# A decoder layer on one core: head outputs and the output weights of the first attention as fp16 high and low parts

## The chip, the cores and the metric

One core of one Trainium2 chip runs the whole layer. The time is device microseconds from launch to end; the median of three runs is compared. The engines are named as in the profile: PE (TensorE, its matmuls), PEld (its weight loads), DVE (VectorE), ACT (ScalarE), POOL (GpSimd) and SP (SyncE, which issues all DMAs of this kernel). PSUM is the matmuls' output memory, SBUF the memory of tiles.

## The reference, cut to what matters

The layer is: latent self-attention with 128 heads of 4 content and 64 rope dimensions, cross-attention with 32 heads, a feed-forward layer with LoRA experts, each behind a layer norm and with a residual sum. x is 8 x 128 x 512, fp32. What is changed is the last line of the first attention:

```python
    scores = (einsum('bqhd,bkhd->bhqk', q_c, k_c) + einsum('bqhd,bkd->bhqk', q_r, k_r)) / scale
    attn = jax.nn.softmax(scores, axis=-1)
    out = jnp.einsum('bhqk,bkhd->bqhd', attn, v_c)
    out = out.reshape(b, s, N_HEADS * HEAD_DIM)      # 512 columns
    return out @ Wo                                  # 512 x 512, then x = x + this
```

## The kernel before

**The loop over half steps.** The 128 heads go in 32 groups of 4 (`g`), each in two half steps (`t` = 0, 1) of four batches, so there are 64 half steps `h = 2g + t`. In half step h, PE projects the rope queries of job h (24 matmuls in 8 pieces, `project`), computes rough scores of job h-1 in four pieces (`rough_scores`, L1547) and full scores of job h-2 (L1580, L1581), turns the row maxima of job h-1 (`max_turn`, L1557) and weighs the values of job h-3 (L1595). All engines run the same half steps, each in its own written order, tied by semaphores. A job's scores need its row maxima back as a row of the query tile QC: DVE takes the maxima (`row_max`, L1095), PE turns them, DVE writes them to mT (`max_out`, L1164), and SP copies mT into QC.

**DVE in a half step** (`half`): `q_low` of job h-1, chunk 1 (two L1083), `o_out` (L1170), four `row_max` (L1095), `q_low` of job h, chunk 0 (two L1083), and last `max_out` of job h-1. PE's third rough piece of a half step waits for the first `row_max` of the same half step, since they share two PSUM banks. **ACT in a half step**: `q_high` of job h-1, chunk 1, four casts to Ph (L935), four exponentials (L928), with `q_high` of job h, chunk 0 among them. **POOL** forms Pl, the low part of the probabilities (L653, four in each half step), and in each even half step splits the next group's weights: `high` (L628), after the Pl of one job `rest` (L632, L634), then a copy of values (L639).

**The normalisation of head outputs.** Jobs store unnormalised outputs and softmax sums to HBM; SP gathers them per quarter T of the heads (32 heads, 128 rows) into U (outputs, turned, fp32) and SU (sums). DVE takes the reciprocal of SU and multiplies, 128x128 for each of eight batches b. The table `shares(h)` places these: `inverse_sums` (L1202) among the row maxima, `apply_sums` (L1207) behind the second `q_low`, ahead of `max_out`. Quarter 0 falls on half steps 26 to 33, quarter 1 on 42 to 49, quarter 2 on 58 to 63 and just behind. Quarter 3 is done by `normalise` (L1213, L1214) after the last half step and, for batches 4 to 7, within the cross-attention.

**The product with Wo.** `output_part(v, T)` (L1620) and `output(v, T)` (L1629) multiply U by the fp32 weights wo_sb: 32 products of 128x128 by 128x512. The first twelve stand between the rough and full scores of the last jobs; then come eight for batches 0 and 1, eight for 2 and 3, and four single ones in the cross-attention. `x1_part` and `x1` add them to the residual xs; norm statistics and `norm_rows` (tile pn) of the next layer norm follow on DVE.

**The code of each engine** is either written out (`spelled`) or a hardware loop of two groups per pass (`looped`). DVE and ACT have groups 1 and 2 written out and loop from 3.

## Time and profile before

| what | value |
|---|---|
| median of 3 runs | 836.3 us (836.21 to 837.79) |
| the profiled execution | 836.2 us, its span 834.5 us |
| PE busy | 795.2 us, 95% |
| DVE busy | 627.3 us, 75% |
| POOL busy | 590.8 us, 71% |
| ACT busy | 582.8 us, 70% |
| mean granted TensorE clock | 0.997 |

The span is the time between the first and the last instruction, and 1.7 us lie around it. Busy time is summed over the span. Rows of the timeline give the start, the length, the engine, the line and the operation; the bracket behind is idle time of the engine ahead of the row, and what ended it. An instruction that has been issued and waits inside the engine for a port has a longer row and no bracket.

### The profile page before, as it was taken

What the parts mean: (1) busy time and instruction counts of PE and PEld (TensorE: products, weight loads), DVE (VectorE), ACT (ScalarE), POOL (GpSimd) and SP (SyncE); (2) the same over time, 40 slices, a digit from 0 to 9 for tenths busy, and PEclk for the clock granted to TensorE, in tenths of its full rate; (3) what the DMA queues carried; (4) which work ended last, traced back from release to release, by engine and by line L of the source; (5) the groups of instructions that cost most, each with busy time, mean ns of one, the idle gap of its engine ahead of it and who ended that gap; (6) DMA issues with size and microseconds to landing.
All of it is one profiled execution on the core that took longest, in us unless ns stands there. A gap on an engine that the chain in (4) does not pass through costs nothing.

```text
span 834.5 us, 17885 instructions
## 1 busy us (share of the span) xinstructions
PE 795.2 (95%) x5641; PEld 391.1 (47%) x5641; DVE 627.3 (75%) x1189; ACT 582.8 (70%) x1072; POOL 590.8 (71%) x535
## 2 busy tenths in 40 slices
PE   5999999999999999999999999999999888999986
PEld 3464444444444444444444444444434434545443
DVE  6767676676766888767788877688868868888755
ACT  8757777777777778777777777768765556556641
POOL 6967999999987888878888788868657334222110
PEclk9999999999999999999999999999999999999999
DMA  9345355534343333433334434452322000000001
GB/s 339 124 170 146 88 160 145 171 82 97 101 123 103 79 95 84 117 106 91 102 88 93 106 91 105 100 153 56 81 57 65 2 2 2 14 14 15 15 14 38
DMA packets 52177, 75.80 MB, mean 91 GB/s; under 512 B 10257, under 2 KB 34097, under 8 KB 51617
## 3 DMA queue, kind: packets, MB, share of 16 engines
q1 hardware_dynamic: 52128, 75.23, 32.8%
q8 instruction: 22, 0.36, 0.2%
q14 instruction: 27, 0.21, 0.1%
HBM read 38.69 MB, written 19.40 MB: 70 GB/s over the span
## 4 chain that ended last, share of the span: by engine, by line
PE 82%; DVE 7%; ACT 4%; issue 3%; SPq 2%; DMA 1%; POOL 0%; DVEq 0%; ACTq 0%
PE PS L1508 38%; PE PS L1442 7%; PE PS L1547 7%; PE PS L1580 7%; PE PS L1581 6%; PE PS L1595 5%; DVE xm L1281 1%; PE PS L1620 1%; PE PS L1741 1%; PE PS L1557 1%; PE PS L1707 1%; PE PS L1815 1%; PE PS L1629 1%; SPq L464 1%; PE PS L1748 1%
## 5 line engine op out<-in xcount | busy, mean ns | idle before, releaser
L1508 PE MATMUL PS<-XTh,W 128*128 128x512 f16 x1024 | 346.2, 379 | 0.0
L653 POOL TENSOR_TENSOR Pl<-PR,Ph 128x512 f16<-128x512 f32 x254 | 286.3, 1159 | 29.8 <-ACT Ph L935 29.8
L928 ACT ACTIVATE PR<-PS 128x512 f32<-128x512 f32 x256 | 152.8, 597 | 129.5 <-PE PS L1581 122.6
L1095 DVE TENSOR_REDUCE mneg<-PS 128x4 f16<-128x512 f32 x256 | 171.6, 685 | 34.7 <-PE PS L1547 33.0
L1508 PE MATMUL PS<-XTl,W 128*128 128x512 f16 x512 | 193.8, 379 | 0.0
L1083 DVE SCALAR_TENSOR_TENSOR QS<-PS,QC 64x512 f16<-64x512 f32 x256 | 175.4, 685 | 20.9 <-ACT QC L845 16.8
L845 ACT ACTIVATE QC<-PS 64x512 f16<-64x512 f32 x256 | 150.7, 589 | 9.2 <-PE PS L1508 4.3
L1508 PEld LDWEIGHTS PS<-XTh,W 128*128 128x128 f16 x1024 | 96.5, 97 | 118.8 <-issue 25.9
L935 ACT ACTIVATE Ph<-PR 128x512 f16<-128x512 f32 x256 | 139.2, 617 | 0.0
L1547 PEld LDWEIGHTS PS<-KC,QC 112*128 112x128 f16 x1024 | 78.4, 97 | 63.5 <-DVE mneg L1095 2.8
L1547 PE MATMUL PS<-KC,QC 112*128 112x128 f16 x1024 | 99.5, 219 | 0.8 <-ACT QC L845 0.7
L1580 PE MATMUL PS<-QC,KC 113*128 113x512 f16 x256 | 97.8, 382 | 2.1 <-DMA QC<-mT 1.6
L1581 PE MATMUL PS<-QS,KS 128*128 128x512 f16 x256 | 97.3, 380 | 0.0
L628 POOL TENSOR_TENSOR W<-Wraw,wscale 128x1024 f16<-128x1024 f32 x30 | 56.8, 1893 | 46.2 <-PE PS L1508 40.6
L1508 PEld LDWEIGHTS PS<-XTl,W 128*128 128x128 f16 x512 | 49.8, 97 | 46.3
L1164 DVE TENSOR_SCALAR mT<-PS 16x128 f16<-16x128 f16 x64 | 13.6, 212 | 76.7 <-PE PS L1557 76.7
L784 POOL TENSOR_TENSOR rstd<-rstd,power 128x1 f32<-128x1 f32 x16 | 8.8, 553 | 82.4 <-DVE rstd L1260 82.4
L634 POOL TENSOR_TENSOR W<-Wraw,W 128x1024 f16<-128x1024 f32 x30 | 64.0, 2133 | 2.4
L632 POOL TENSOR_TENSOR Wraw<-Wraw,wscale 128x1024 f32<-128x1024 f32 x30 | 56.8, 1892 | 0.2
L1170 DVE COPY OS<-PS 128x512 f32<-128x512 f32 x64 | 44.2, 691 | 4.1 <-PE PS L1595 2.2
L1281 DVE TENSOR_REDUCE xm<-PS 128x4 f16<-128x512 f32 x64 | 41.0, 682 | 2.0 <-PE PS L1707 2.0
L1595 PE MATMUL PS<-Ph,Vg 128*32 128x512 f16 x512 | 41.4, 383 | 0.0
(229 smaller groups left out, 1032.4 us busy)
## 6 DMA issues: line engine op xcount, KB each, us to landing
Wraw<-in_wqr SPq DMA_DIRECT2D x32, 512.0 KB, 4.8
QS<-QC SPq DMA_DIRECT2D x64, 256.0 KB, 3.1
head_outputs<-OS SPq DMA_DIRECT2D x256, 40.0 KB
q_content_parts<-stg SPq DMA_DIRECT2D x12, 256.0 KB, 2.9
k_content_parts<-stg SPq DMA_DIRECT2D x12, 256.0 KB, 3.1
QC<-q_content_parts SPq DMA_DIRECT2D x116, 24.0 KB
KC<-k_content_parts SPq DMA_DIRECT2D x29, 96.0 KB
xs<-in_x SPq DMA_DIRECT2D x8, 256.0 KB, 5.2
```

What stands on the lines that cost most here:

```text
L634: nc.gpsimd.tensor_tensor(Wl[:, par], Wraw[:, par], Wh[:, par], ALU.subtract).then_inc(s_ws, 1)
L653: nc.gpsimd.tensor_tensor(Pl[:, 4 * j.s + b], PR[:, b], Ph[:, 4 * j.s + b], ALU.subtract).then_inc(s_pl, 1)
L845: nc.scalar.activation(QC[0:RD, j.p, j.s, 2 * c + h, :], PS[RD * h:RD * (h + 1), bQ[c], :], ACT.Copy, scale=1 / WS).then_inc(s_qh, 1)
L928: nc.scalar.activation(PR[:, b, :], PS[:, bB[b % 2], :], ACT.Exp, scale=ATT_SCALE).then_inc(s_e, 1)
L935: nc.scalar.activation(Ph[:, 4 * j.s + b, :], PR[:, b, :], ACT.Copy).then_inc(s_ph, 1)
L1083: nc.vector.scalar_tensor_tensor(QS[0:RD, j.p, j.s, i, :], PS[RD * h:RD * (h + 1), bQ[c], :], 1 / WS, QC[0:RD, j.p, j.s, i, :], ALU.mult, ...
L1095: nc.vector.tensor_reduce(mneg[:, j.p, j.s, :, b], PS[:, bA[b % 2], :].rearrange("p (j k) -> p j k", j=GH), AX.X, ALU.max, negate=True).th ...
L1508: last = mm(PS[:, bQ[c], :], wt[:, j.w, k, c * P:(c + 1) * P], xt[:, k, sl], start=(i == 0), stop=(i == 3 * KT - 1))
L1547: last = mm(PS[:, bA[i % 2], h * S:(h + 1) * S], QC[0:MROW, j.p, j.s, h, i * S:(i + 1) * S], kc(j.k)[0:MROW, b * S:(b + 1) * S], start=Tru ...
L1580: mm(to, kc(j.k)[0:MROW + 1, b * S:(b + 1) * S], QC[0:MROW + 1, j.p, j.s, :, i * S:(i + 1) * S], start=True, stop=False)
L1581: mm(to, KS[:, b * S:(b + 1) * S], QS[:, j.p, j.s, :, i * S:(i + 1) * S], start=False, stop=True).then_inc(s_b, 1)
L1595: last = mm(PS[32 * b:32 * (b + 1), bO, :], Vg[:, j.p, part, 4 * j.s + b, :], probs[:, 4 * j.s + b, :], start=(n == 0), stop=(n == 2))
```

## The change

wo_sb goes; in its place stand wo_h and wo_l, fp16, of together the same size. The weights land in bw_raw; at the end of half steps 9 and 10 ACT writes half of wo_h (128x1024) and DVE then writes half of wo_l, ahead of its `max_out`. The feed-forward weights, which used bw_raw too, are loaded as before but wait for wo_l. U is read as fp16 pairs in place (Uparts): DVE multiplies into SU, casts to the high part and subtracts for the low part. In the last quarter ACT casts (`u_high`) and DVE subtracts (`u_low`). Each fp32 product becomes three fp16 ones: high by wo_h, high by wo_l, low by wo_h, and the residual sum multiplies by 1/WS. ACT and DVE have groups 1 to 6 written out and loop from 7.

```diff
         scratch = top[0]
-        wo_sb = sb("wo_sb", [P, KT, DM])
+        wo_h = sb("wo_h", [P, KT, DM], F16)
+        wo_l = sb("wo_l", [P, KT, DM], F16)
         wx_raw = sb("wx_raw", [P, KT, DM])
...
         SU = sb("SU", [P, TOK])
+        Uparts = U[:].rearrange("p k t -> p (k t)").bitcast(F16).rearrange("p (k b n s) -> p k b n s", k=KT, n=2, s=S)
         KC2 = sb("KC2", [P, 2, TOK], F16)
...
         s_wdh, s_wds = sem("wd_high"), sem("wd_split")
-        s_c, s_ce, s_cl, s_kc = sem("c_ready"), sem("c_high"), sem("c_low"), sem("k_copied")
+        s_c, s_kc = sem("c_ready"), sem("k_copied")
+        s_ce, s_cl = sem("high_of_c_wo_and_last_u"), sem("low_of_c_wo_and_last_u")
         s_u, s_uh, s_ul, s_uv = sem("up_ready"), sem("up_high"), sem("up_low"), sem("v_high")
...
             sp.wait_ge(s_vl, B)
-            for g, (t, d, done) in enumerate(((wo_sb, wo, s_wo), (wx_raw, xwq, s_wx), (xwo_sb, xwo, s_ffn), (bw_raw, bw, s_ffn))):
+            for g, (t, d, done) in enumerate(((bw_raw, wo, s_wo), (wx_raw, xwq, s_wx), (xwo_sb, xwo, s_ffn), (bw_raw, bw, s_ffn))):
                 spelled(half, 3 + g, 3 + g)
+                if g == 3:
+                    sp.wait_ge(s_cl, 6 + 2)
                 sp.dma_start(t[:], d).then_inc(done, 16)
...
                         q_high(J(0), 0)
-            spelled(half, 1, 2)
-            looped(act, half, 3, G0 - 1)
+                if isinstance(g, int) and 2 * g + t in (9, 10):
+                    k = 2 * (2 * g + t - 9)
+                    act.wait_ge(s_wo, 16)
+                    nc.scalar.activation(wo_h[:, k:k + 2], bw_raw[:, k:k + 2], ACT.Copy, scale=WS).then_inc(s_ce, 1)
+            def u_high(b):
+                act.wait_ge(s_un, B * (KT - 1) + b + 1)
+                nc.scalar.activation(Uparts[:, KT - 1, b, 0], SU[:, b * S:(b + 1) * S], ACT.Copy).then_inc(s_ce, 1)
+            spelled(half, 1, 6)
+            looped(act, half, 7, G0 - 1)
             spelled(half, G0, NG - 1)
...
                 p_high(job(n))
+            u_high(0)
+            u_high(1)
             act.wait_ge(s_red, 2)
...
                 turned_out(u)
+                if u - 1 in SUMS_AT:
+                    u_high(SUMS_AT[u - 1])
                 if r == 2 and 0 <= b + 1 < B:
...
                         split_high(n)
+                    u_high(2)
+                    u_high(3)
                     nc.scalar.activation(ex[:, 0:1], power[:], ACT.Exp)
...
                         apply_sums(*piece)
+                if h in (9, 10):
+                    k = 2 * (h - 9)
+                    dve.wait_ge(s_ce, 6 + h - 8)
+                    nc.vector.scalar_tensor_tensor(wo_l[:, k:k + 2], bw_raw[:, k:k + 2], WS, wo_h[:, k:k + 2],
+                                                   ALU.mult, ALU.subtract).then_inc(s_cl, 1)
                 max_out(J(1))
...
                 dve.wait_ge(s_dch, chain[0])
-                nc.vector.tensor_tensor(U[:, T, sl], U[:, T, sl], SU[:, sl], ALU.mult).then_inc(s_un, 1)
+                link(nc.vector.tensor_tensor(SU[:, sl], U[:, T, sl], SU[:, sl], ALU.mult))
+                link(nc.vector.tensor_copy(Uparts[:, T, b, 0], SU[:, sl]))
+                nc.vector.tensor_tensor(Uparts[:, T, b, 1], SU[:, sl], Uparts[:, T, b, 0], ALU.subtract).then_inc(s_un, 1)
+            def u_low(b):
+                dve.wait_ge(s_ce, 8 + b + 1)
+                nc.vector.tensor_tensor(Uparts[:, KT - 1, b, 1], SU[:, b * S:(b + 1) * S], Uparts[:, KT - 1, b, 0],
+                                        ALU.subtract).then_inc(s_cl, 1)
             def normalise(T, b):
...
                 link(nc.vector.reciprocal(SU[:, sl], SU[:, sl]))
-                nc.vector.tensor_tensor(U[:, T, sl], U[:, T, sl], SU[:, sl], ALU.mult).then_inc(s_un, 1)
-            spelled(half, 1, 2)
-            looped(dve, half, 3, 12)
+                if T < KT - 1:
+                    link(nc.vector.tensor_tensor(SU[:, sl], U[:, T, sl], SU[:, sl], ALU.mult))
+                    link(nc.vector.tensor_copy(Uparts[:, T, b, 0], SU[:, sl]))
+                    nc.vector.tensor_tensor(Uparts[:, T, b, 1], SU[:, sl], Uparts[:, T, b, 0], ALU.subtract).then_inc(s_un, 1)
+                else:
+                    nc.vector.tensor_tensor(SU[:, sl], U[:, T, sl], SU[:, sl], ALU.mult).then_inc(s_un, 1)
+            spelled(half, 1, 6)
+            looped(dve, half, 7, 12)
             spelled(half, 13, 16)
...
                 dve.wait_ge(s_o0, v - B // 2 + 1)
-                nc.vector.tensor_tensor(xs[:, v, :], xs[:, v, :], PS[:, v - B // 2, :], ALU.add).then_inc(s_x0, 1)
+                nc.vector.scalar_tensor_tensor(xs[:, v, :], PS[:, v - B // 2, :], 1 / WS, xs[:, v, :], ALU.mult, ALU.add).then_inc(s_x0, 1)
...
                     dve.wait_ge(s_x0, v - B // 2 + 1)
-                nc.vector.tensor_tensor(xs[:, v, :], xs[:, v, :], PS[:, o1_bank(v), :], ALU.add).then_inc(s_x1, 1)
+                nc.vector.scalar_tensor_tensor(xs[:, v, :], PS[:, o1_bank(v), :], 1 / WS, xs[:, v, :], ALU.mult, ALU.add).then_inc(s_x1, 1)
...
             normalise(KT - 1, 1)
+            u_low(0)
+            u_low(1)
             x1(0)
...
                     normalise(KT - 1, 3)
+                    u_low(2)
+                    u_low(3)
                 if u == FIRST + 3:
...
                     normalise(KT - 1, SUMS_AT[u])
+                if u - 1 in SUMS_AT:
+                    u_low(SUMS_AT[u - 1])
...
+            def residual(bank, v, T, start, stop):
...
+                for n, (part, wt) in enumerate(((0, wo_h), (0, wo_l), (1, wo_h))):
+                    if n == 2 and T == KT - 1:
+                        pe.wait_ge(s_cl, 8 + v + 1)
+                    last = mm(PS[:, bank, :], Uparts[:, T, v, part], wt[:, T, :], start=(start and n == 0), stop=(stop and n == 2))
+                return last
             def output_part(v, T):
...
                 pe.wait_ge(s_un, B * T + v + 1)
-                last = mm(PS[:, v - B // 2, :], U[:, T, v * S:(v + 1) * S], wo_sb[:, T, :], start=(T == 0), stop=(T == KT - 2))
+                last = residual(v - B // 2, v, T, T == 0, T == KT - 2)
                 if T == KT - 2:
...
-                pe.wait_ge(s_un, B * T + v + 1)
+                if T < KT - 1:
+                    pe.wait_ge(s_un, B * T + v + 1)
+                else:
+                    pe.wait_ge(s_ce, 8 + v + 1)
                 if T == 0:
                     pe.wait_ge(s_x0, v + 1)
-                last = mm(PS[:, o1_bank(v), :], U[:, T, v * S:(v + 1) * S], wo_sb[:, T, :], start=(T == 0 or v >= B // 2),
-                          stop=(T == KT - 1))
+                last = residual(o1_bank(v), v, T, T == 0 or v >= B // 2, T == KT - 1)
                 if T == KT - 1:
...
-            pe.wait_ge(s_wo, 16)
+            pe.wait_ge(s_cl, 6 + 2)
             for i in range(4):
...
```

The order of instructions on DVE at the end of half step 26 and the start of 27, the first with a piece of quarter 0 (U the outputs, SU the sums, mneg the row maxima, QS and QC query tiles, OS a job's outputs). Before:

```order
L1095 TENSOR_REDUCE mneg<-PS 128x4 x2
L1083 SCALAR_TENSOR_TENSOR QS<-PS,QC 64x512 x2
L1207 TENSOR_TENSOR U<-U,SU 128x128
L1164 TENSOR_SCALAR mT<-PS 16x128
L1083 SCALAR_TENSOR_TENSOR QS<-PS,QC 64x512 x2
L1170 COPY OS<-PS 128x512
```

and now:

```order
L1114 TENSOR_REDUCE mneg<-PS 128x4 x2
L1102 SCALAR_TENSOR_TENSOR QS<-PS,QC 64x512 x2
L1231 TENSOR_TENSOR SU<-U,SU 128x128
L1232 CAST U<-SU 128x128
L1233 TENSOR_TENSOR U<-SU,U 128x128
L1183 TENSOR_SCALAR mT<-PS 16x128
```

Two instructions more stand between the second `q_low` and `max_out`. The same place in half step 9, now written out:

```order
L1114 TENSOR_REDUCE mneg<-PS 128x4 x4
L1102 SCALAR_TENSOR_TENSOR QS<-PS,QC 64x512 x2
L1218 SCALAR_TENSOR_TENSOR wo_l<-bw_raw,wo_h 128x1024
L1183 TENSOR_SCALAR mT<-PS 16x128
L1102 SCALAR_TENSOR_TENSOR QS<-PS,QC 64x512 x2
```

Before, the loop had the same four without the row of wo_l. DVE behind the last scores, with `normalise` of batches 0 and 1 of quarter 3 and `x1(0)`. Before:

```order
L1170 COPY OS<-PS 128x512
L1213 RECIPROCAL SU<-SU 128x128
L1214 TENSOR_TENSOR U<-U,SU 128x128
L1213 RECIPROCAL SU<-SU 128x128
L1214 TENSOR_TENSOR U<-U,SU 128x128
L1332 TENSOR_TENSOR xs<-xs,PS 128x512
L1258 BN_STATS stats<-xs 128x6
```

and now:

```order
L1189 COPY OS<-PS 128x512
L1245 RECIPROCAL SU<-SU 128x128
L1251 TENSOR_TENSOR SU<-U,SU 128x128
L1245 RECIPROCAL SU<-SU 128x128
L1251 TENSOR_TENSOR SU<-U,SU 128x128
L1237 TENSOR_TENSOR U<-SU,U 128x128 x2
L1369 SCALAR_TENSOR_TENSOR xs<-PS,xs 128x512
```

The two subtractions of `u_low` stand ahead of the residual sum of batch 0.

## Rows read from the trace of the kernel before

**Rows 1.** The page: busy time, share of the span and instructions of each engine.

```profile
PE 795.2 (95%) x5641; PEld 391.1 (47%) x5641; DVE 627.3 (75%) x1189; ACT 582.8 (70%) x1072; POOL 590.8 (71%) x535
```

**Rows 2.** PE's timeline 155 to 174: turns of the row maxima (start, length).

```profile
155.43 0.22 PE L1557 MATMUL PS<-turns,mneg 128*16 128x128 f16 x1
...
164.17 0.22 PE L1557 MATMUL PS<-turns,mneg 128*16 128x128 f16 x1
...
173.13 0.22 PE L1557 MATMUL PS<-turns,mneg 128*16 128x128 f16 x1
```

**Rows 3.** DVE's timeline 155 to 167: the first `q_low` of two half steps.

```profile
156.16 1.41 DVE L1083 SCALAR_TENSOR_TENSOR QS<-PS,QC 64x512 f16<-64x512 f32 x2 [0.26 <-ACT QC L845]
...
165.28 1.41 DVE L1083 SCALAR_TENSOR_TENSOR QS<-PS,QC 64x512 f16<-64x512 f32 x2 [0.55 <-ACT QC L845]
```

**Rows 4.** The chain that ended last, 690 to 834.5: two stretches.

```profile
751.81 2.59 PE PS L1442 x12
754.40 0.86 PE PS L1815 x2
```

**Rows 5.** Groups by line and form: busy us, mean ns | idle before.

```profile
L1629 PE MATMUL PS<-wo_sb,U 128*128 128x512 f32 x40 | 18.8, 601 | 0.2 <-DVE U L1214 0.2
...
L1207 DVE TENSOR_TENSOR U<-U,SU 128x128 f32<-128x128 f32 x23 | 12.9, 564 | 0.0
...
L1620 PE MATMUL PS<-wo_sb,U 128*128 128x512 f32 x24 | 12.6, 605 | 0.0
...
L1244 DVE SCALAR_TENSOR_TENSOR Wxl<-wx_raw,Wxh 128x2048 f16<-128x2048 f32 x1 | 2.3, 2285 | 0.0
...
L945 ACT ACTIVATE W<-Wraw 128x1024 f16<-128x1024 f32 x2 | 2.1, 1050 | 3.1 <-DMA Wraw<-in_wqr 3.1
```

**Rows 6.** DVE's timeline 277 to 288: behind half steps 26 and 27.

```profile
277.17 1.09 DVE L1207 TENSOR_TENSOR U<-U,SU 128x128 f32<-128x128 f32 x1
278.65 0.21 DVE L1164 TENSOR_SCALAR mT<-PS 16x128 f16<-16x128 f16 x1 [0.39 <-PE PS L1557]
279.12 1.41 DVE L1083 SCALAR_TENSOR_TENSOR QS<-PS,QC 64x512 f16<-64x512 f32 x2 [0.26 <-ACT QC L845]
...
287.38 0.21 DVE L1164 TENSOR_SCALAR mT<-PS 16x128 f16<-16x128 f16 x1 [1.20 <-PE PS L1557]
```

**Rows 7.** POOL's timeline 276 to 281.

```profile
276.22 1.89 POOL L632 TENSOR_TENSOR Wraw<-Wraw,wscale 128x1024 f32<-128x1024 f32 x1
278.19 2.13 POOL L634 TENSOR_TENSOR W<-Wraw,W 128x1024 f16<-128x1024 f32 x1
280.26 0.45 POOL L639 COPY Vg<-V 128x320 f16 x1
```

**Rows 8.** DVE's timeline 568 to 571: end of half step 59.

```profile
569.11 0.32 DVE L1207 TENSOR_TENSOR U<-U,SU 128x128 f32<-128x128 f32 x1
569.76 0.21 DVE L1164 TENSOR_SCALAR mT<-PS 16x128 f16<-16x128 f16 x1 [0.33 <-PE PS L1557]
```

**Rows 9.** POOL's timeline 568 to 572.

```profile
569.36 1.16 POOL L664 TENSOR_TENSOR W<-Wraw,W 128x512 f16<-128x512 f32 x1
```

**Rows 10.** ACT's timeline 128 to 129: end of half step 9.

```profile
128.13 0.60 ACT L928 ACTIVATE PR<-PS 128x512 f32<-128x512 f32 x1 [0.49 <-PE PS L1581]
```

**Rows 11.** DVE's timeline 117 to 150: `max_out` of half steps 9 and 10.

```profile
129.03 0.21 DVE L1164 TENSOR_SCALAR mT<-PS 16x128 f16<-16x128 f16 x1 [1.49 <-PE PS L1557]
...
138.31 0.21 DVE L1164 TENSOR_SCALAR mT<-PS 16x128 f16<-16x128 f16 x1 [1.49 <-PE PS L1557]
```

**Rows 12.** POOL's timeline 128 to 131.

```profile
128.88 1.89 POOL L628 TENSOR_TENSOR W<-Wraw,wscale 128x1024 f16<-128x1024 f32 x1 [1.03 <-issue]
```

**Rows 13.** DVE's timeline 623 to 628.

```profile
624.70 1.25 DVE L1214 TENSOR_TENSOR U<-U,SU 128x128 f32<-128x128 f32 x1
...
627.16 0.69 DVE L1332 TENSOR_TENSOR xs<-xs,PS 128x512 f32<-128x512 f32 x1
```

**Rows 14.** POOL's timeline 585 to 668.

```profile
623.53 4.62 POOL L653 TENSOR_TENSOR Pl<-PR,Ph 128x512 f16<-128x512 f32 x4 [2.49 <-ACT Ph L935]
```

## The prediction

> **What bounds the kernel now.** I read the page first: PE is busy for 95% of the span, DVE for 75% [rows 1]. Then PE's timeline at the one instruction that comes once in a half step, the turn of the row maxima: two stand 8.74 us apart [rows 2], which most of the 64 half steps repeat, and PE has no gap in between. So the loop is PE's, and in a half step that lasts longer another engine ends a wait last. How little is spare shows the next turn, 8.96 us behind [rows 2]: in that half step DVE began its first `q_low` 1.11 us after the turn instead of 0.73 [rows 2, 3], at a place where its loop jumps back. DVE was 0.38 us late and PE lost 0.22. The order explains it: behind `q_low` come `o_out` and the first `row_max`, and PE's third rough piece waits for that one. So **what delays DVE's end of a half step by more than 0.16 us costs PE the rest.** The 0.4 to 1.5 us that DVE idles before `max_out` are the only cover.
>
> **What the products gain.** An fp32 product is two matmul rows that take 0.86 us together, 0.43 each; twelve fp16 ones of 512 columns take 2.59 us, 0.216 each [rows 4]. Three of those take 0.65, so each of the 32 products (64 rows of L1620 and L1629 [rows 5]) takes 0.21 less: 6.8 us of PE time at most. Twelve stand among the last scores, where PE is the bound: 12 x 0.21 = 2.5. I take 2.2, since the first three are followed by rough pieces that wait for row maxima. The other twenty stand where DVE is next (below).
>
> **What the normalisation costs in the loop.** DVE had one multiplication for each piece. It now has a chain of three: multiplication, cast, subtraction. The last is of the multiplication's kind and size, 0.3 us when alone. Of such a cast there is no row; it lies between nothing and that 0.3, and I take 0.2, since it reads one tile less. In an odd half step that is 0.5 more against 1.20 us of idle time before `max_out` [rows 6]: no cost. In an even one the multiplication lasts 1.09 us and only 0.39 stay idle [rows 6]. The cause is on POOL's timeline: L632 runs from 276.22 to 278.11 [rows 7], and the multiplication, issued at 277.17, ends at 278.26, 0.15 behind it. Over all 23 its mean is 0.564 [rows 5]: that is eight of 1.04 (the even half steps of quarters 0 and 1) and fifteen of 0.3. So a DVE instruction with both inputs in SBUF waits until the POOL instruction that runs is done.
>
> The Trainium skill (SBUF — State Buffer, "Who interferes with whom") says that the two engines share one pair of ports, held for a whole instruction, and that a DVE instruction with two SBUF inputs contends with POOL's reads. By the same section a cast in a two-port mode contends too. The first is what the row shows; for the second no row of before exists. By the rule the second end below holds, 2.2 us for each piece.
>
> At 278.19 POOL starts L634, 2.13 us, to 280.32, and at its end the copy L639, 0.45 us [rows 7]. The multiplication's row ends at 278.26, so nothing of the chain gets ahead of L634. The two ends of the cost:
> - Only the subtraction waits: it ends at 280.32 + 0.15 = 280.47 and `max_out` follows at once (before: 278.65). `q_low` starts 0.25 us after that, at 280.75 instead of 279.12 [rows 6]: 1.63 late, 1.5 for PE.
> - The cast, issued at 278.3, waits as the multiplication did: it ends at 280.45, L639 may get in between (to 280.9), the subtraction ends at 281.2, `q_low` starts at 281.45: 2.3 late, 2.2 for PE.
>
> I take **2.0 us in each of eight even half steps, 16 us**, range 12 to 17.5; it is nearer the second end, as the cast is issued under L634 just as the multiplication is under L632. It repeats, since POOL's part of an even half step begins when PE is done with a projection: a stall of PE moves both. The maxima's way into QC is late by the same amount and lies beside the same stall.
>
> Quarter 2 meets other work of POOL. In half step 59 the multiplication starts at 569.11, lasts 0.32, and `max_out` starts at 569.76; POOL has L664 from 569.36 to 570.52 [rows 8, 9] and the next of the pair of about the same length behind it. Cast behind the first, subtraction behind the second: done at 571.8, 2.0 after the old `max_out`, 1.9 for PE. Half step 58 is alike, but the one behind it waits for transfers already: 0.3. Half step 62 does two pieces, 1.0 more against 0.4 of idle time: 0.4. Half steps 60, 61 and 63 have cover. Together **2.6**, range 1 to 3.5.
>
> **What splitting the weights costs.** At the end of half step 9 ACT's last exponential ends at 128.73 [rows 10]. Behind it comes the cast of wo_h, 1.05 us by the row of its size [rows 5], to 129.8. DVE, which did `max_out` at 129.03 [rows 11], waits for it, and then for POOL's L628, 128.88 to 130.77 [rows 12], two SBUF inputs again. A subtraction of this form over 2048 columns took 2.29 us [rows 5], 1.2 for half of it. It ends at 131.95, `max_out` is 2.9 late. PE then loses 2.7 us, of which 0.55 were lost there before (9.28 between two `max_out`, the first jump back of DVE's loop [rows 11]): 2.1 net. At half step 10 POOL has got behind and holds nothing at that moment: ACT 1.1 and DVE 1.2 us behind the turn, 2.0 late, 1.9 for PE. Together **4.0**, range 2.5 to 4.7. That the loops start at group 7 takes away two jumps back (half steps 10 and 14) and makes that of half step 18 the first: nothing on balance. The later load of the feed-forward weights costs nothing: SP comes to it when DVE is past half step 10, and their first reader stands behind the loop.
>
> **The end of the first attention.** Behind the twelve products DVE is next. The multiplication of batch 0 lasts 1.25 us under POOL's four Pl, which go on from 623.53 to 628.15, and `x1(0)` starts at 627.16 [rows 13, 14]. Now two subtractions stand ahead of it, the first held by the fourth Pl: `x1(0)` at 628.75, **1.6** later, and the norm, the query projection and the cross-attention are behind it. For batches 2 and 3 the subtractions wait for ACT, which has three weight splits ahead of its casts, and for POOL: between 0.6 (their own length) and 2.2 (two of POOL's instructions of 1.1), I take **1.5**; PE's faster products there are hidden by DVE. Batches 4 to 7 give DVE 0.3 more and PE 0.21 less each: **0.3** in all. Less the 2.2 gained, this end costs 1.2, range -2 to 3.
>
> **Sum.** 16 + 2.6 + 4.0 + 1.2 = 23.8 us on the 836.2 of the profiled execution: 860. The median of the three runs is 0.1 higher, which changes nothing. With all ends of the terms: 850 to 865.
>
> **Rivals.**
> - *Only the subtraction is held* (the cast runs beside POOL). Eight times 1.5 instead of 2.0: 856. For it: the cast reads one tile. Chance 0.28, against 0.55 for the forecast as it stands.
> - *DVE's chain slips past POOL.* For it: the multiplication of batch 0 got in between two Pl instructions of POOL [rows 13, 14]. If cast and subtraction took the 0.08 us between L632 and L634 and held L634 off, an even half step would be late by 0.5 - 0.39, under 0.16: nothing. Against it: L634 begins before the multiplication's row ends. Left are 4.0 for the weights, 0.5 in quarter 2 and 1.2: 842. Chance 0.07.
> - *The saving on PE decides: faster.* One mechanism: DVE's additions stay hidden. It decides where DVE is less than 0.16 us late at half steps 9 and 10 and at the ten even pieces; then 6.8 are left, 829, or the 2.2 alone, 834. For it: 25% of DVE's span is idle. Against it: that idle time is 0.39 where it counts. Chance 0.06.
> - *A second stall behind the first*: late maxima also keep SP from its stores and content loads, and the next half step stalls as well. One more microsecond at ten places: 870. Against it: no row shows a half step in which SP's queue is the one waited for. Chance 0.04.
>
> **How the numbers follow.** The forecast is 860, its own range 853 to 866. For 8 in 10 the range takes in the case of the subtraction alone and part of the last: 848 to 868. A change under 0.2% (1.7 us) is about what a measurement of this kernel can't tell from none. Slower 0.9, the same 0.04 (cases that cancel), faster 0.06.
>
> **What would show it.** In the profile after, the turn of half step 27 comes 10.7 us behind that of 26 instead of 8.74, likewise behind each even half step of quarters 0 and 1, and 8.74 behind the odd ones. In the even ones the cast's row lasts about 2 us, to L634's end (or the subtraction's, in the second case). At half step 9 DVE's `wo_l` row lasts over 2 us. PE is idle ahead of L1547 for DVE's row maxima. The products of 0.65 us show as shorter stretches among the last scores. The forecast is wrong if DVE's chain in an even half step ends before L634 does, or if PE's third rough piece has more slack than the 0.16 us that I read from one late half step.

## The result, and the profile after

| | before | after |
|---|---|---|
| median of 4 runs each, side by side | 837.0 us (836.2 to 840.0) | 858.3 us (856.3 to 862.2) |
| ratio | | 1.026 (1.0236 to 1.0284) |
| profiled execution, its span | 836.2, 834.5 us | 856.3, 854.6 us |

The changed kernel is 2.6% slower. The page's busy times beside [rows 1]:

```profile
PE 790.5 (93%) x5673; PEld 387.2 (45%) x5673; DVE 664.1 (78%) x1247; ACT 585.8 (69%) x1082; POOL 591.2 (69%) x535
```

PE is busy for 4.7 us less and DVE for 36.8 us more (rows in which DVE waits for POOL count as busy), in a span that is 20.1 us longer. In PE's timeline the turns of the row maxima (now L1600) show where the time went. These are the turns and the waits of PE for row maxima in the changed kernel, 127 to 151 and 280 to 300 us:

```profile
128.49 0.22 PE L1600 MATMUL PS<-turns,mneg 128*16 128x128 f16 x1
134.62 0.40 PE L1590 MATMUL PS<-KC,QC 112*128 112x128 f16 x4 [1.99 <-DVE mneg L1114]
139.69 0.22 PE L1600 MATMUL PS<-turns,mneg 128*16 128x128 f16 x1
144.89 0.40 PE L1590 MATMUL PS<-KC,QC 112*128 112x128 f16 x4 [1.06 <-DVE mneg L1114]
149.78 0.22 PE L1600 MATMUL PS<-turns,mneg 128*16 128x128 f16 x1
...
280.83 0.22 PE L1600 MATMUL PS<-turns,mneg 128*16 128x128 f16 x1
286.25 0.40 PE L1590 MATMUL PS<-KC,QC 112*128 112x128 f16 x4 [1.39 <-DVE mneg L1114]
291.13 0.22 PE L1600 MATMUL PS<-turns,mneg 128*16 128x128 f16 x1
299.87 0.22 PE L1600 MATMUL PS<-turns,mneg 128*16 128x128 f16 x1
```

The intervals behind half steps 9 and 10 are 11.20 and 10.09 us, the one behind half step 26 is 10.30, the one behind 27 is 8.74 as before [rows 2]. Each of the long ones, and each one behind the other even half steps of quarters 0 and 1, has an idle stretch of PE (1.06 to 1.99 us) that a row maximum ended. Taken over all turns and the first events behind them, the 20.1 us are:

| stretch | more than before | forecast |
|---|---|---|
| up to half step 9 | -0.2 | 0 |
| behind half steps 9 and 10 (the weights) | +3.3 | +4.0 |
| behind half steps 13, 17 and 21 (the jumps back) | -0.6 | 0 |
| behind the eight even half steps of quarters 0 and 1 | +12.1 | +16 |
| quarter 2, half steps 57 to 62 | +1.3 | +2.6 |
| last scores, PE's faster products | -2.2 | -2.2 |
| to the residual sum of batch 0 | +1.6 | +1.6 |
| to the first turned queries of the cross-attention (KQ) | +1.4 | +1.5 |
| cross-attention and feed-forward | +3.4 | +0.3 |

DVE's timeline of the changed kernel at the end of half steps 27 and 28, beside [rows 6]:

```profile
290.02 0.28 DVE L1231 TENSOR_TENSOR SU<-U,SU 128x128 f32<-128x128 f32 x1
290.33 0.23 DVE L1232 CAST U<-SU 128x128 f16<-128x128 f32 x1
290.59 0.29 DVE L1233 TENSOR_TENSOR U<-SU,U 128x128 f16<-128x128 f32 x1
291.39 0.21 DVE L1183 TENSOR_SCALAR mT<-PS 16x128 f16<-16x128 f16 x1 [0.51 <-PE PS L1600]
...
298.65 0.99 DVE L1231 TENSOR_TENSOR SU<-U,SU 128x128 f32<-128x128 f32 x1
299.68 2.10 DVE L1232 CAST U<-SU 128x128 f16<-128x128 f32 x1
301.82 0.42 DVE L1233 TENSOR_TENSOR U<-SU,U 128x128 f16<-128x128 f32 x1
302.27 0.21 DVE L1183 TENSOR_SCALAR mT<-PS 16x128 f16<-16x128 f16 x1
```

and POOL's at the same place, beside [rows 7]:

```profile
297.60 1.90 POOL L637 TENSOR_TENSOR Wraw<-Wraw,wscale 128x1024 f32<-128x1024 f32 x1
299.57 2.12 POOL L639 TENSOR_TENSOR W<-Wraw,W 128x1024 f16<-128x1024 f32 x1
301.64 0.45 POOL L644 COPY Vg<-V 128x320 f16 x1
```

In the odd half step the three instructions take 0.8 us and `max_out` (L1183) still waits 0.51 us for PE. In the even one the same cast has a row of 2.10 us that ends 0.1 us behind POOL's L639 (301.69). The subtraction is issued right behind it, under POOL's copy (L644), and ends at 302.24, 0.15 us behind the end of the copy (302.09): it waits too. All eight even half steps of quarters 0 and 1 show these two distances.

### The profile page after: what moved, and what is told of

Same layout as the page of the kernel before. It is cut to its first block, busy times and chain, and to the rows that moved or that the text cites. A ratio compares the mean times of both kernels' runs of the same rounds, so it can differ in the third digit from the quotient of the medians.

```text
span 854.6 us, 17905 instructions
## 1 busy us (share of the span) xinstructions
PE 790.5 (93%) x5673; PEld 387.2 (45%) x5673; DVE 664.1 (78%) x1247; ACT 585.8 (69%) x1082; POOL 591.2 (69%) x535
## 4 chain that ended last, share of the span: by engine, by line
PE 71%; DVE 16%; ACT 4%; issue 4%; SPq 2%; DMA 1%; POOL 0%; DVEq 0%; ACTq 0%
PE PS L1551 32%; PE PS L1485 7%; PE PS L1590 6%; PE PS L1623 6%; PE PS L1624 6%; PE PS L1638 4%; DVE QS L1102 3%; DVE U L1232 2%; DVE mneg L1114 2%; PE PS L1795 1%; PE PS L1665 1%; DVE OS L1189 1%; PE PS L1761 1%; DVE SU L1231 1%; PE PS L1600 1%
## 5 line engine op out<-in xcount | busy, mean ns | idle before, releaser
L1102 DVE SCALAR_TENSOR_TENSOR QS<-PS,QC 64x512 f16<-64x512 f32 x256 | 175.3, 685 | 15.7 <-ACT QC L850 11.7
L1590 PEld LDWEIGHTS PS<-KC,QC 112*128 112x128 f16 x1024 | 77.4, 97 | 81.9 <-DVE mneg L1114 23.8
L639 POOL TENSOR_TENSOR W<-Wraw,W 128x1024 f16<-128x1024 f32 x30 | 63.9, 2131 | 2.4
L1183 DVE TENSOR_SCALAR mT<-PS 16x128 f16<-16x128 f16 x64 | 13.6, 212 | 61.6 <-PE PS L1600 61.2
```

The costliest lines, as they stand in the source:

```text
L639: nc.gpsimd.tensor_tensor(Wl[:, par], Wraw[:, par], Wh[:, par], ALU.subtract).then_inc(s_ws, 1)
L1102: nc.vector.scalar_tensor_tensor(QS[0:RD, j.p, j.s, i, :], PS[RD * h:RD * (h + 1), bQ[c], :], 1 / WS, QC[0:RD, j.p, j.s, i, :], ALU.mult, ...
L1590: last = mm(PS[:, bA[i % 2], h * S:(h + 1) * S], QC[0:MROW, j.p, j.s, h, i * S:(i + 1) * S], kc(j.k)[0:MROW, b * S:(b + 1) * S], start=Tru ...
```

## The experiments

Nine edits, in four comparisons; one of the kernels was run twice. The first three take the even half steps apart.

**Without the cast.**

```diff
-                link(nc.vector.tensor_copy(Uparts[:, T, b, 0], SU[:, sl]))
-                nc.vector.tensor_tensor(Uparts[:, T, b, 1], SU[:, sl], Uparts[:, T, b, 0], ALU.subtract).then_inc(s_un, 1)
+                nc.vector.tensor_tensor(Uparts[:, T, b, 1], SU[:, sl], SU[:, sl], ALU.add).then_inc(s_un, 1)
...
```

> Left out: the cast of the 23 pieces that the loop normalises; the subtraction is replaced by an addition of the same tile to itself (both inputs in SBUF, as before), and PE reads its result for both parts in these pieces, so the output is not the layer's. Theory A (a DVE instruction with two SBUF inputs waits for the POOL instruction that runs): the addition alone waits for the rest of POOL's 2.13 us instruction in the eight even half steps of quarters 0 and 1 and lasts about 2 us there; PE loses 1.1 to 1.3 us behind each (1.5 in the changed kernel). Rival B (what costs is the chain's own time and its semaphores): one instruction of 0.3 us against 0.39 us of idle time, PE loses nothing behind even half steps.

Measured: 854.0 us, one run. The intervals behind the eight even half steps are 9.92 and 9.81 in turn, 1.18 and 1.07 more than 8.74. So the chain with one instruction less still waits for POOL: the addition ends 0.15 us behind the end of POOL's L639 (302.62), and what is saved is the work behind that wait. DVE's and POOL's rows of this kernel in half step 28:

```profile
300.60 2.17 DVE L1232 TENSOR_TENSOR U<-SU 128x128 f16<-128x128 f32 x1
302.80 0.21 DVE L1183 TENSOR_SCALAR mT<-PS 16x128 f16<-16x128 f16 x1
```

```profile
300.49 2.13 POOL L639 TENSOR_TENSOR W<-Wraw,W 128x1024 f16<-128x1024 f32 x1
```

**Reduces in place of the cast and the subtraction.**

```diff
-                link(nc.vector.tensor_copy(Uparts[:, T, b, 0], SU[:, sl]))
-                nc.vector.tensor_tensor(Uparts[:, T, b, 1], SU[:, sl], Uparts[:, T, b, 0], ALU.subtract).then_inc(s_un, 1)
+                link(nc.vector.tensor_reduce(U[:, T, b * S:b * S + 4], SU[:, sl].rearrange("p (j k) -> p j k", j=4), AX.X, ALU.max))
+                nc.vector.tensor_reduce(U[:, T, b * S + 4:b * S + 8], SU[:, sl].rearrange("p (j k) -> p j k", j=4), AX.X, ALU.max).then_inc(s_un, 1)
...
```

> Cast and subtraction of the 23 pieces in the loop are replaced by two chained reductions over the same 128x128 tile, one SBUF input each, and PE reads a stand-in tile for these pieces, so the output is not the layer's. Theory A (waiting for POOL): reductions do not wait, the chain is 0.6 us longer than before the change in an even half step, of which 0.39 us are idle time and the rest is within the slack of 0.16 to 0.35 us: turns of the row maxima 8.74 us apart, 8.9 at most, behind even half steps; the span is 11 to 12 us shorter than the changed kernel's. Rival B (the chain's own time and links): 10.2 to 10.3 us, as in the changed kernel.

Measured: 849.7 us, one run, span 847.9. Behind the even half steps 8.74 stands again (9.11 behind the first, 8.80 behind one other). DVE's rows of this kernel in half step 26:

```profile
281.51 1.09 DVE L1231 TENSOR_TENSOR SU<-U,SU 128x128 f32<-128x128 f32 x1
282.64 0.29 DVE L1232 TENSOR_REDUCE U<-SU 128x4 f32<-128x128 f32 x1
282.96 0.29 DVE L1233 TENSOR_REDUCE U<-SU 128x4 f32<-128x128 f32 x1
283.27 0.21 DVE L1183 TENSOR_SCALAR mT<-PS 16x128 f16<-16x128 f16 x1
```

The multiplication waits as ever, and two further instructions of together 0.6 us do not, though POOL's second long instruction runs. A reduce writes only 4 columns, so this run alone doesn't show that the full work would be free; the next one does. At the last turn, turn 64, this kernel is 10.0 us ahead of the changed one (616.10 against 626.10), and would be 11.7 ahead, as expected, without a stretch at half rate in half step 9 (12.86 us instead of 11.20, below). The whole span gains only 6.7: behind turn 64 this profile has four stretches at half rate and that of the changed kernel one.

**The split moved to odd half steps.** The even half step only multiplies; the odd one casts and subtracts both batches.

```diff
                         apply_sums(*piece)
+                    if h - 1 in KEPT:
+                        split_sums(*shares(h - 1)[0], *shares(h)[0])
...
+            KEPT = tuple(range(26, 34, 2)) + tuple(range(42, 50, 2)) + (59,)
+            def split_sums(T, a, _, b):
+                for part in range(2):
+                    for v in (a, b):
...
+                h = b + 16 * T + 26
+                if h in KEPT or h - 1 in KEPT:
+                    ins = nc.vector.tensor_tensor(SU[:, sl], U[:, T, sl], SU[:, sl], ALU.mult)
...
```

> All work is kept; cast and subtraction of the eight even pieces of quarters 0 and 1 and of half step 59 are done at the end of the next half step, where POOL is idle, together with those of that half step's own piece. DVE's chain there is 0.5 us longer than in the changed kernel. Theory A (waiting for POOL): behind even half steps 8.74 us again, at most 0.15 us lost behind odd ones, 1.3 us less behind half step 59: 12 to 13.5 us less than the changed kernel, 843 to 845. Rival B (own time): the work is the same and only moves, the odd half steps now lose what the even ones lost, 856 to 858.

Measured: 846.6 us, ratio to before 1.010 (1.0074 to 1.0127). Behind the sixteen half steps of quarters 0 and 1 all intervals are 8.73 or 8.74 but two (9.30 and 8.86), and the one behind half step 59 is 8.73 instead of 10.00. Turn 64 is at 614.50, 11.6 us ahead of the changed kernel. DVE's rows of this kernel in the odd half step 27:

```profile
290.04 0.36 DVE L1238 CAST U<-SU 128x128 f16<-128x128 f32 x2
290.32 0.49 DVE L1241 TENSOR_TENSOR U<-SU,U 128x128 f16<-128x128 f32 x2
291.21 0.21 DVE L1183 TENSOR_SCALAR mT<-PS 16x128 f16<-16x128 f16 x1 [0.40 <-PE PS L1623]
```

Both pieces are split in 0.8 us, and `max_out` still waits for PE. All the work is done here, and DVE's chain costs PE nothing: in the interval of 9.30 us, behind half step 26, DVE is on time and PE waits 0.39 us for the transfer of mT into QC, and in both runs of the kernel with three fixes (below) all sixteen are 8.73 or 8.74. The time is 1.6 us above the upper end of what theory A expected, and far from theory B's 856 to 858.

**The last quarter of batches 4 to 7 by DVE alone.** The table above leaves 3.4 us in a stretch for which 0.3 was forecast. The changed kernel's timeline at the splits of one of these batches, all engines, 711 to 736 us:

```profile
717.12 0.31 ACT L972 ACTIVATE U<-SU 128x128 f16<-128x128 f32 x1 [3.74 <-DVE SU L1251]
717.91 0.25 ACT L1010 ACTIVATE xmT<-PS 8x128 f16<-8x128 f16 x1
718.30 0.38 PE L1751 MATMUL PS<-turns,qst 128*128 128x128 f16 x4 [1.20 <-ACT xmT L1010]
...
723.40 0.28 DVE L1237 TENSOR_TENSOR U<-SU,U 128x128 f16<-128x128 f32 x1
723.74 0.39 PE L1665 MATMUL PS<-wo_h,U 128*128 128x512 f16 x1 [1.33 <-DVE U L1237]
```

`u_high` stands on ACT right behind the eviction of turned queries and waits for DVE's multiplication, which comes at the end of DVE's unit; `xmT`, queued behind it, is late and PE idles 1.20 us. One unit later PE idles 1.33 us more, with its third product waiting for `u_low`. The edit drops both and lets `normalise` cast and subtract on DVE:

```diff
-                if u - 1 in SUMS_AT:
-                    u_high(SUMS_AT[u - 1])
...
-                if T < KT - 1:
+                if T < KT - 1 or b >= B // 2:
...
-                if u - 1 in SUMS_AT:
-                    u_low(SUMS_AT[u - 1])
...
```

> Batches 4 to 7 of the last quarter are cast by DVE itself within the normalisation, as in quarters 0 to 2; ACT has no cast for them and the subtraction no longer stands at the end of the next unit. Theory C (in the cross-attention ACT stands in its queue for the normalisation, which DVE does at the end of the unit, and PE's last product of the batch stands for a subtraction one unit later): about 2.6 us for each of batches 6 and 7 go away, and some for 4 and 5: 3 to 4.5 us less than the changed kernel, 853 to 855. Rival D (the added DVE and ACT time itself): DVE gets 0.23 us more for each, the time is the same or up to 1 us longer.

Measured: 854.3 us, ratio to before 1.021 (1.0188 to 1.0232). ACT's evictions of the turned queries (KQ), counted from 0, in this kernel and in the changed one, each against before, in us:

| KQ number | 3 | 6 | 9 | 15 | 19 | 31 |
|---|---|---|---|---|---|---|
| changed kernel | 16.71 | 17.20 | 15.52 | 17.76 | 19.89 | 19.90 |
| batches 4 to 7 by DVE | 17.77 | 17.91 | 16.23 | 16.84 | 17.42 | 17.43 |

Only the steps from one number to the next tell here, since ahead of number 3 the two profiles differ by a stretch at half rate. The steps of 0.5, 2.2 and 2.1 us become 0.1, 0.6 and 0.6. The fall of 1.68 at number 9 is in both and is not the change's (below).

**The weights in odd half steps.** Four pieces of half the size; ACT's also moves, ahead of the exponentials, and SP loads the feed-forward weights later, once all four are split.

```diff
-                if isinstance(g, int) and 2 * g + t in (9, 10):
-                    k = 2 * (2 * g + t - 9)
+                if isinstance(g, int) and 2 * g + t in (9, 11, 13, 15):
+                    k = (2 * g + t - 9) // 2
                     act.wait_ge(s_wo, 16)
-                    nc.scalar.activation(wo_h[:, k:k + 2], bw_raw[:, k:k + 2], ACT.Copy, scale=WS).then_inc(s_ce, 1)
+                    nc.scalar.activation(wo_h[:, k:k + 1], bw_raw[:, k:k + 1], ACT.Copy, scale=WS).then_inc(s_ce, 1)
...
-            spelled(half, 1, 6)
-            looped(act, half, 7, G0 - 1)
+            spelled(half, 1, 8)
+            looped(act, half, 9, G0 - 1)
...
```

> The changed kernel, with the output weights split in four pieces of 128x512 instead of two of 128x1024, in the odd half steps 9, 11, 13 and 15 in place of 9 and 10; ScalarE's piece stands right behind its first high part of the probabilities, where the next rough scores' reduces are not yet due, and the two engines' loops begin at half step 9 instead of 7. Everything is computed as in the changed kernel. Theory A: the 3.27 us that half steps 9 and 10 cost in the changed kernel (turn intervals 11.20 and 10.09 into h10 and h11, against 9.29 and 8.74 before) are ScalarE's 1.05 us piece ahead of the queries' eviction and VectorE's wait of 2.17 us for it, which holds up the reduces of the rough scores and so TensorE; in odd half steps with pieces of half the size most of it is gone: -2.5 to -3.3 us against the profiled changed kernel, each of the intervals behind 9, 11, 13 and 15 at most 9.0. Theory B: the weights' work costs the same wherever it stands, because VectorE and ScalarE are full there: the four intervals together are 3 us longer than 4 x 8.74, and the time is that of the changed kernel within 0.5 us. Beside either, in some profiles TensorE runs about 3 us at half its clock behind the wait of 1.99 us in half step 10 (1.66 us lost: the runs without the cast and with SyncE-free tail show it, the changed kernel's own does not); with the wait gone that can't come, so against a median that holds it up to 1.7 us more.

Measured: 854.4 us, ratio to before 1.020 (1.0172 to 1.0227), against 1.026. All intervals from half step 9 to 16 are 8.73 or 8.74. DVE's rows of this kernel in half step 9:

```profile
126.86 0.72 DVE L1220 SCALAR_TENSOR_TENSOR wo_l<-bw_raw,wo_h 128x512 f16<-128x512 f32 x1
128.34 0.21 DVE L1185 TENSOR_SCALAR mT<-PS 16x128 f16<-16x128 f16 x1 [0.76 <-PE PS L1602]
```

and the corresponding ones of the changed kernel:

```profile
129.52 2.15 DVE L1218 SCALAR_TENSOR_TENSOR wo_l<-bw_raw,wo_h 128x1024 f16<-128x1024 f32 x1 [2.17 <-ACT wo_h L968]
131.71 0.21 DVE L1183 TENSOR_SCALAR mT<-PS 16x128 f16<-16x128 f16 x1
```

The work of one piece now ends before `max_out` is due. Size, half step and place on ACT were changed together, so that the share of each is not shown. ("The run with SyncE-free tail" in the expectation is the one with batches 4 to 7 by VectorE.)

**The loops alone.** The kernel before with one edit:

```diff
-            spelled(half, 1, 2)
-            looped(act, half, 3, G0 - 1)
+            spelled(half, 1, 6)
+            looped(act, half, 7, G0 - 1)
...
-            spelled(half, 1, 2)
-            looped(dve, half, 3, 12)
+            spelled(half, 1, 6)
+            looped(dve, half, 7, 12)
```

> The kernel before with one thing of the change alone: the half steps 1 to 6 of ScalarE and VectorE are written out, and their loops begin at half step 7 instead of 3. Nothing else differs. Theory A: the jump back of the two loops is on the path where it lies (turn intervals 9.29 at h10 and 8.96, 8.95, 8.94 at h14, 18 and 22 in the kernel before, against 8.74 elsewhere), and since the loops' jumps now fall in other half steps where they are hidden, the changed kernel's gain of 0.63 us at h14 to h22, and 0.55 more at h10, comes from this alone: the time falls by 0.6 to 1.2 us (0.1 per cent). Theory B: jumps cost the same wherever they stand, and only the one jump fewer counts: -0.2 to -0.5 us. Theory C, the prediction's: nothing on balance.

Measured: 836.7 us in 12 runs against 838.1 in 22, ratio 0.9987 (0.9968 to 1.0006): by the times it can't be told from no change. The intervals tell: 9.29, 8.96, 8.95 and 8.94 behind half steps 9, 13, 17 and 21 of the kernel before are 8.73 or 8.74, all four, 1.2 us in sum. PE's timeline of this kernel, beside [rows 11] and [rows 2]:

```profile
128.22 0.22 PE L1557 MATMUL PS<-turns,mneg 128*16 128x128 f16 x1
136.95 0.22 PE L1557 MATMUL PS<-turns,mneg 128*16 128x128 f16 x1
```

**All three fixes together**: weights in odd half steps, splits in odd half steps, batches 4 to 7 by DVE, put together from the diffs above. It ran twice, in two comparisons.

> The changed kernel with three edits together: the weights are split in four small pieces in odd half steps 9 to 15 (as above), the heads' outputs of two even-odd batches are split by VectorE in the odd half step behind the products (as in the run that did this alone), and the last quarter's outputs of batches 4 to 7 are split by VectorE alone as they are normalised (as in the run that did this alone). Everything is computed. If the three parts are independent, as theory A says, the terms add: 836.5 for the profiled kernel before, -0.6 for the loops, about 0 for the weights, -0.1 for quarters 0 to 2 (intervals of 8.73 against 8.74), +1.4 for batches 2 and 3 and +1.2 for the cross-attention that remain: 838 to 839, so the time is that of the kernel before within 0.4 per cent, and 18 to 20 us below the changed one. Theory B: the parts cover for one another (VectorE is at 78 per cent and now has all of it to do), and one of them takes back what the others give: 841 or more.

> The kernel with the three edits together, once more, so that the one with the last quarter by VectorE alone is compared with it on one chip. Expected: 836.2 as before within 0.1 per cent if the chip is the same, and a ratio to the kernel before of 0.998.

Measured: 836.2 us and 0.9978 (0.9965 to 0.9991) of the kernel before in the first, 836.9 us and 0.9993 (0.9981 to 1.0006) in the second, a little more than the 0.998 expected of it. The whole 2.6% is gone; a gain on the kernel before beyond 0.2% is not shown. Not every part of the loss is: the 1.6 us up to the residual sum of batch 0 and 1.3 in the cross-attention stay, against the 2.2 that PE's products gain and what the jumps gave. The time is 1 to 3 us below the sum of theory A: the jumps gave 1.0 instead of 0.6, and the 1.4 for batches 2 and 3 were mostly half rate (below), which is not in every run.

**The whole last quarter by DVE.**

```diff
-            u_high(0)
-            u_high(1)
...
-            u_low(0)
-            u_low(1)
...
-                if T < KT - 1 or b >= B // 2:
-                    link(nc.vector.tensor_tensor(SU[:, sl], U[:, T, sl], SU[:, sl], ALU.mult))
+                link(nc.vector.tensor_tensor(SU[:, sl], U[:, T, sl], SU[:, sl], ALU.mult))
...
```

> The kernel with the three edits together (the weights in four pieces in odd half steps, the splits in odd half steps, the last quarter of batches 4 to 7 split by VectorE alone), and in it the last quarter of batches 0 to 3 split by VectorE alone too: multiply, cast and subtraction behind each other for each batch, and TensorE waits once instead of for ScalarE's high part and again for VectorE's low part. In that kernel the two waits are 1.23 and 1.40 us for batches 0 and 1 and 1.05 us for batches 2 and 3, and behind the second of them TensorE's products run at half rate for some 3 us (0.63 us instead of 0.38 us each; about 1.3 us lost). Theory A: the waits for two engines in turn are the cost of batches 0 to 3, and VectorE's own cast (0.3 us) is shorter than the hand-over: the first of batch 0's products starts no later, x1 of batch 0 is 1 to 3 us earlier, and the turned queries of the first unit of the cross-attention 1.5 to 3 us earlier than in that kernel (643.01): 833 to 835 in a run that is undisturbed, 0.2 to 0.4 per cent below it. Theory B: GpSimd runs in this stretch (the multiply of batch 0 took 1.24 us instead of 0.29), so that VectorE's cast waits as it did in the even half steps (2.10 us), and the time is the same or up to 1 us longer.

Measured: 840.5 us, ratio to before 1.0039 (1.0022 to 1.0055), against 836.9 for the kernel that it starts from, on the same chip: 0.4% slower. Theory B's mechanism, and more than the 1 us that it allowed. DVE's rows of this kernel for batch 0, POOL's, and PE's wait:

```profile
623.73 1.24 DVE L1265 TENSOR_TENSOR SU<-U,SU 128x128 f32<-128x128 f32 x1
625.00 1.06 DVE L1266 CAST U<-SU 128x128 f16<-128x128 f32 x1
626.09 1.14 DVE L1267 TENSOR_TENSOR U<-SU,U 128x128 f16<-128x128 f32 x1
```

```profile
622.55 4.53 POOL L660 TENSOR_TENSOR Pl<-PR,Ph 128x512 f16<-128x512 f32 x4 [1.35 <-ACT Ph L942]
```

```profile
627.29 0.41 PE L1673 MATMUL PS<-wo_h,U 128*128 128x512 f16 x1 [3.15 <-DVE U L1267]
```

POOL has four Pl of 1.13 us each behind each other here (622.55 to 627.08), and each instruction of the chain waits for one of them; PE's single wait of 3.15 us is longer than its two of 1.24 and 1.40 in the kernel with three fixes. For batch 2 the cast and the subtraction take 1.13 and 1.03 us in the same way. The same edit that gained 3.5 us at batches 4 to 7, where DVE's rows for batches 5 to 7 show no wait (0.29, 0.23 and 0.29 us) and batch 4's 0.2 us, loses here.

**The order of PE's products.**

```diff
             for v in range(2):
-                for T in range(KT):
+                for T in range(KT - 1):
                     output(v, T)
+            for v in range(2):
+                output(v, KT - 1)
```

> The kernel with the three edits together, and the order of TensorE's products for batches 0 and 1 changed: the nine products of quarters 0 to 2 of batch 1 stand ahead of the three of the last quarter of batch 0, in whose waits (1.23 and 1.40 us) they then lie. The profiles of the kernel with the three edits show TensorE at half rate behind the second wait in one (626 to 629 us; 33.06 us from turn 64 to the first turned queries) and at full rate in the other (31.95 us), against 31.81 in the kernel before and 33.08, with half rate at 642 to 645, in the changed kernel. Theory A: the half rate comes behind TensorE's idle time, and with 1.9 us of products in it there is no half-rate stretch here in any profile, and 31.8 to 32.0 us from turn 64 to the first turned queries; the mean gain over the kernel with the three edits is 0.3 to 0.8 us (0.1 per cent), at the limit of what the runs tell: 0.997 to 0.999 of the kernel before. Theory B: the order is no matter, since batch 0's last product and not batch 1's sets what follows, and the half rate comes in some runs all the same: 0.9985, as the two runs of the kernel with the three edits together.

Measured: 838.1 us, ratio to before 1.0009 (0.9994 to 1.0025). Theory A falls: the profile has a stretch at half rate (629.5 to 633 us), and 32.15 us from turn 64 to the first turned queries. The ratio is also a little above theory B's 0.9985. PE's timeline of this kernel:

```profile
624.68 0.60 PE L1686 MATMUL PS<-wo_h,U 128*128 128x512 f16 x2 [0.86 <-DVE U L1260]
...
628.38 0.65 PE L1835 MATMUL PS<-ident,pn 128*128 128x128 f32 x4 [2.67 <-DVE pn L1327]
...
630.69 1.06 PE L1686 MATMUL PS<-wo_h,U 128*128 128x512 f16 x2
```

The first idle stretch is 0.86 us instead of 1.24, and the second is filled, but what follows waits for DVE's `pn` all the same, so that the rest of the idle time stands in one piece of 2.67 us, and behind it the products run at half rate.

## Why the prediction was right, point by point

The forecast was 860 us, the time 858.3. The profiled execution is 20.1 us longer than before where 23.8 were forecast, and the terms were not all right: three were too large and one much too small.

**The even half steps, 16 us forecast, 12.1 found.** The mechanism is the one forecast, in its second form: the cast, issued under POOL's long instruction, waits for its end (2.10 us), and the subtraction for the copy's. With the cast left out an addition of the subtraction's kind waits in its place; reduces, which don't wait, bring 8.74 back; and the same work in odd half steps is free. The size was off by three allowances. From the end of the cast to that of the subtraction it is 0.46 us where 0.75 was allowed, since the subtraction ends 0.15 behind the copy and not its own 0.3; `q_low` starts 0.17 us behind the subtraction's end, not 0.25; and PE has more slack than the forecast gave it. In half step 28 `q_low` starts at 302.41, 2.54 us behind the turn, where 0.73 is the undisturbed distance: 1.81 us late. PE lost 1.46 there. So PE's slack is some 0.35 and not the 0.16 that was read from one late half step [rows 2, 3].

**Quarter 2, 2.6 forecast, 1.3 found**, nearly all of it behind half step 59 (10.00 us instead of 8.73). "Half step 62 does two pieces", at 0.4, measured 0.16. At half step 59 cast and subtraction each wait for one POOL instruction, as forecast, and `max_out` is 1.9 us late (2.0 forecast); `q_low`, which closes up to it, is only 1.6 late, and the slack takes the rest. Half step 58 cost nothing: the next one waits 1.20 us for a row maximum where before it waited 1.43 for transfers.

**The weights, 4.0 forecast.** The two intervals are 3.3 us longer, but the 9.29 of before held 0.55 of a jump back that is no longer there; against 8.74 they are 2.46 and 1.35 longer, 3.8 in all, where 2.7 and 1.9 were forecast. At half step 9 `wo_l` waits for ACT (2.17 us) and then for POOL (its row is 2.15 us long, against 1.23 at half step 10). So the cause is right and the size 0.7 too large; with the pieces halved and put in odd half steps nothing is left.

**"That the loops start at group 7 [is] nothing on balance"** was wrong by 0.6 us: the jumps at half steps 9, 13, 17 and 21 cost 1.2 us before, of which the forecast had counted the 0.55 at half step 9, and in the changed kernel and in the one with the loops alone none that remain costs anything to be seen. Why is open: the jumps behind half steps 17 and 21 are still there, as the first and the second of the loop. With the loops from half step 18 on (the weights in odd half steps, and the kernels built on it) the first one, behind 21, costs 0.16.

**The end of the first attention, 1.2 forecast, 4.2 found.** Three of its four parts had the right size: -2.2 up to the last scores' end, +1.6 for `x1(0)`, and +1.4 for 1.5 behind it, this last one for a wrong reason. Only about 0.25 of it is the order of DVE: from `x1(0)` to KQ number 0 it takes 15.31 us before, 15.56 in the second run of the kernel with three fixes, which has the changed kernel's order here and runs at full rate, and 16.66 in the changed kernel, where PE's products run at half rate at 642 to 645 us behind its waits of 1.22 and 1.40 us. The fourth, "batches 4 to 7: 0.3 in all", is **the step that failed**. It counted DVE's 0.3 and not that each batch now crosses from DVE to ACT and back to DVE, with `xmT` queued on ACT behind the wait and PE's third product behind the second crossing. It costs 4.9 us: 0.5, 2.2 and 2.1 at three places, with one batch hidden. With DVE alone 1.3 are left. The profile shows 3.4, since 1.7 us of half rate that the profile of before has at 676 to 680 us happen to be absent in that of the changed kernel.

So the mechanism that decides the result was right, and that the sum came so near was in part luck: 3.9 us too many in the even half steps, 1.3 in quarter 2, 0.7 for the weights and 0.6 for the jumps stood against 4.6 too few in the cross-attention, of which the clock hid 1.7. The rival with only the subtraction held (856) was nearly as near in time, and wrong: the cast waits.

## What to carry to other kernels

A DVE cast, with one input, was held by POOL just as an instruction with two, and a reduce was not: look which POOL instruction runs at the place before adding a cast there, and put the work where POOL's stretch is empty or its instructions short. Here three such changes of place made 21 us of loss vanish without leaving out any work. Work that goes from one engine to another and back is priced by the two hand-overs and by what is queued behind each wait, not by its length. And where forecast and time agree, compare the terms: a sum of 23.8 that measures 20.1 held two errors of some 5 us with opposite signs.

## What the runs showed of the hardware

**A cast from fp32 to fp16 in SBUF waits for POOL.** Of the 23 casts of 128x128 in the changed kernel those beside an idle POOL took 0.23 us and those issued as POOL's L639 began 2.10, ending some 0.08 us behind it; the mean is 0.97. A subtraction or an addition with both inputs in SBUF ended 0.15 us behind the POOL instruction that it waited for. A reduce of the same tile took 0.29 us beside the same instruction. The Trainium skill (SBUF — State Buffer, "Who interferes with whom") says that a cast in a two-port mode contends with GpSimd, and the rows of 2.10 us agree; that the cast ran in such a mode no row shows.

**TensorE's clock falls behind idle time, in some runs.** Behind the wait of 1.99 us in half step 9 the changed kernel's own profile shows full clock, and that of the kernel without the cast, with the same wait, shows half: windows of the two (core 0: us, PE, PEld, DVE, ACT, POOL busy, PEclk, DMA share, GB/s).

```profile
134.50:139.00 4.50, 4.37 (x26) 2.17 (x27) 3.24 (x6) 2.86 (x5) 4.42 (x4) 1.00 0.40 98
```

```profile
134.50:139.00 4.50, 4.50 (x18) 2.00 (x17) 2.82 (x5) 2.26 (x4) 4.42 (x4) 0.62 0.43 106
```

Products that start 0.216 us apart at 2.4 GHz start 0.43 apart there, at 1.2 GHz, for some 3 us: 1.66 us lost (12.86 instead of 11.20 to the next turn). Of the five profiles that have this wait three show the stretch and two do not. The same happened in the kernel before, whose window at 676 us is

```profile
676.00:680.00 4.00, 4.00 (x21) 1.82 (x19) 0.00 (x0) 0.31 (x1) 0.84 (x1) 0.62 0.02 4
```

behind a wait of 1.89 us, and not in the kernel with the loops alone, whose gain at KQ number 9 is 1.68 us larger for it. The spread of a kernel's runs follows this in part: in the two comparisons of the kernel with three fixes, the six runs at a mean granted clock of 1.000 took 832.8 to 835.5 us, and the eight at 0.992 and 0.993 took 835.3 to 838.2. Another part lies in the start: in the twelve profiles the first turn of row maxima comes at 58.7 to 62.4 us. What decides whether the clock falls behind a given wait stays open. A single profile of each kernel therefore tells a step of 1.7 us at one place only when the clock there is the same in both.
